# Graph layer with LayerNorm on one core: LayerNorm sums moved from ScalarE to VectorE, one rectification four tiles wide moved, other warming products

## The reference

```
h   = max((x - mean(x)) / sqrt(var(x) + 1e-5), 0)      x: 8192 x 128, mean and var over the 128 columns
out = x + relu(adj @ (h @ W) + b)                      adj: 8192 x 8192 dense float32, W: 128 x 128
```

## Time and profile before

| | |
|---|---|
| median of 3 runs | 722.23 us (722.19 to 722.49) |
| the profiled execution's own time | 722.6 us |
| its span | 720.8 us |
| PE, DVE, ACT, POOL busy | 99%, 86%, 72%, 24% of the span |
| transferred | 281.60 MB, mean 391 GB/s |

### The profile page before, as it was taken

One profiled execution on the slowest core, in us unless ns is written; L12 is line 12 of the kernel. 1 busy time (PEld: TensorE's weight loads), 2 busy tenths in 40 slices (PEclk: granted clock), 3 DMA queues, 4 the chain that ended last, 5 costly groups with the idle time before them and its releaser, 6 DMA issues.

```text
span 720.8 us, 7916 instructions
## 1 busy us (share of the span) xinstructions
PE 715.5 (99%) x3125; PEld 586.4 (81%) x3125; DVE 620.4 (86%) x387; ACT 517.0 (72%) x394; POOL 171.5 (24%) x99
## 2 busy tenths in 40 slices
PE   9999999999999999999999999999999999999998
PEld 5788888888888888888888888888888888888886
DVE  5899999999999888988789888878888787888885
ACT  2798988888888867766567677677676676766662
POOL 4445455554444402222011000000000000033213
PEclk9999999999999999999999999999999999999999
DMA  9999999999999999999999999999999999999992
GB/s 352 408 409 407 408 412 415 412 416 415 416 414 416 418 415 412 398 374 402 373 412 392 408 409 389 377 401 383 386 392 373 389 394 387 391 404 397 366 400 85
DMA packets 45109, 281.60 MB, mean 391 GB/s; under 512 B 5136, under 2 KB 5776, under 8 KB 31504
## 3 DMA queue, kind: packets, MB, share of 16 engines
q1 hardware_dynamic: 44496, 280.25, 97.5%
q10 hardware_dynamic: 576, 0.85, 0.4%
HBM read 276.89 MB, written 4.19 MB: 390 GB/s over the span
## 4 chain that ended last, share of the span: by engine, by line
PE 97%; DMA 2%; DVE 0%; ACT 0%; SPq 0%; issue 0%; DVEq 0%
PE banks L558 94%; DMA raw<-adj 2%; PE banks L600 2%; PE banks L592 1%; PE banks L585 0%; PE banks L586 0%; PE banks L584 0%; ACT high L378 0%; SPq L244 0%; DVE x_sb L479 0%; DVE x_sb L487 0%; DVEq L150 0%; DVE warm L491 0%; DVEq L478 0%
## 5 line engine op out<-in xcount | busy, mean ns | idle before, releaser
L516 DVE TENSOR_TENSOR low<-raw,high 128x3072 fp32r<-128x3072 f32 (+2 forms) x255 | 574.7, 2276 | 86.4 <-PE banks L558 64.4
L378 ACT ACTIVATE high<-raw 128x3072 fp32r<-128x3072 f32 (+2 forms) x255 | 483.0, 1903 | 190.3 <-DMA raw<-adj 178.4
L558 PE MATMUL banks<-high,h_high 128*128 128x512 f32 x1012 | 271.6, 390 | 1.1 <-ACT high L378 1.1
L558 PE MATMUL banks<-high,h_low 128*128 128x512 f32 x1012 | 271.0, 389 | 0.0
L558 PE MATMUL banks<-low,h_high 128*128 128x512 f32 x1012 | 267.8, 389 | 0.0
L558 PEld LDWEIGHTS banks<-high,h_high 128*128 128x128 f32 x1012 | 189.8, 188 | 41.8 <-ACT high L378 2.0
L558 PEld LDWEIGHTS banks<-low,h_high 128*128 128x128 f32 x1012 | 189.8, 188 | 39.9 <-DVE low L516 0.4
L558 PEld LDWEIGHTS banks<-high,h_low 128*128 128x128 f32 x1012 | 189.9, 188 | 39.5
L330 POOL TENSOR_SCALAR x_sb<-x_sb,bias 128x512 f32<-128x512 f32 x16 | 49.5, 3095 | 419.3 <-DMA x_sb<-x_blocks 419.3
L321 POOL TENSOR_SCALAR z_sb<-x_sb,neg_mean,rstd 128x128 f32<-128x128 f32 x60 | 89.8, 1510 | 1.6
L306 POOL TENSOR_TENSOR rstd<-var_eps,minus_half 128x4 f32<-128x4 f32 (+2 forms) x17 | 31.6, 1861 | 118.3 <-DVE var_eps L421 109.1
(11 more groups left out here) (34 smaller groups left out, 50.1 us busy)
## 6 DMA issues: line engine op xcount, KB each, us to landing
raw<-adj SPq DMA_DIRECT2D x106, 1536.0 KB, 8.9
raw<-adj SPq DMA_DIRECT2D x82, 768.0 KB, 10.5
raw<-adj SPq DMA_DIRECT2D x69, 512.0 KB, 11.8
x_sb<-x_blocks SPq DMA_DIRECT2D x16, 256.0 KB, 8.6
out_blocks<-x_sb SPq DMA_DIRECT2D x15, 256.0 KB, 9.7
x_sb<-x SPq DMA_DIRECT2D x14, 256.0 KB, 11.9
raw<-adj SPq DMA_DIRECT2D x3, 256.0 KB, 6.9
raw<-adj ACTq DMA_DIRECT2D x1, 256.0 KB, 2.7
```

What stands on the lines that cost most here:

```text
L378: nc.scalar.activation(high[:, t % HIGH_SLOTS, cols], raw[:, t % RAW_SLOTS, cols], ACT.Copy).then_inc(high_ready, 1)
L516: nc.vector.tensor_tensor(low[:, t % LOW_SLOTS, cols], raw[:, t % RAW_SLOTS, cols], high[:, t % HIGH_SLOTS, cols].bitcast(F32), ALU.subtra ...
L558: return nc.tensor.matmul(banks[:, FIRST_BANK[g] + c, :], h[:, (t - FIRST_STEP[g]) * DEPTHS[g] + k, :], tile[:, slot, at:at + BANK], start ...
```

## The change

All batches' sums are taken with bn_stats on DVE. From batch 4 on, one tile is summed at the end of each of four steps, the first of them the step at which the mean stood (load_step), and bn_aggr, var_eps and neg_mean follow the fourth. ACT's squares, DVE's mean and variance and their semaphores go. Batch 3 (tiles 8 to 11) is rectified at step 5 in place of step 7; all other rectifications keep their steps. The split of h_first moves from step 9 to step 28. The eight zero products of 128 columns become two of 448 columns, in memory shared with last_sum, which is filled by two memsets; PE waits for both, ACT for the first.

```diff
-SUMMED_BY_DVE = 4
+SUMMED_AHEAD = 4
...
-WARMING = 8
+WARMING, WARM = 2, 448
...
-def batch_at(t, phase, ahead):
-
-    j = t // 4 + ahead
-    return j if t >= FOUR_PASS and t % 4 == phase and j < len(BATCHES) else None
-
-
-def mean_at(t):
-    return batch_at(t, 1, 3) if t >= 5 else None
-
-
-def variance_at(t):
-    return batch_at(t, 3, 3) if t >= 7 else None
+def load_step(j):
+
+    return (j - 3) * 4 + 1
+
+
+def load_at(t):
+    return next((j for j in range(SUMMED_AHEAD, len(BATCHES)) if load_step(j) == t), None)
+
+
+def summed_at(t):
+
+    for j in range(SUMMED_AHEAD, len(BATCHES)):
+        if load_step(j) <= t < load_step(j) + 4:
+            return j, BATCHES[j][0] + t - load_step(j)
+    return None
 
 
 def rectified_at(t):
-    return 2 if t == 2 else batch_at(t, 3, 2) if t >= 7 else None
-
-
-def squares_at(t):
...
+
+    if t in (2, 5):
+        return 2 if t == 2 else 3
+    j = t // 4 + 2
+    return j if t % 4 == 3 and SUMMED_AHEAD <= j < len(BATCHES) else None
...
+        warm = last_sum[:, 0:WARM]
...
-                if mean_at(t) is not None:
-                    load_x(mean_at(t))
+                if load_at(t) is not None:
+                    load_x(load_at(t))
...
                 pool.wait_ge(rstd_ready, j + 1)
-                if j < SUMMED_BY_DVE:
-                    pool.wait_ge(centre_ready, j + 1)
+                pool.wait_ge(centre_ready, j + 1)
...
-            def square(j, tiles):
...
-                if squares_at(t) is not None:
-                    square(*squares_at(t))
...
-            def mean(j):
...
-            def variance(j):
...
+            def sums_of(j, t):
+                if t == BATCHES[j][0]:
+                    if j == 0:
+                        dve.wait_ge(x_first_landed, 16)
+                    else:
+                        dve.wait_ge(x_landed[x_slot(j)], x_landed_count(j))
+                cols = slice(t % 4 * P, t % 4 * P + P)
+                nc.vector.bn_stats(stats[:, t, :], x_sb[:, x_slot(j), cols]).then_inc(stats_ready, 1)
+
+            def moments_of(j):
                 first, end = BATCHES[j]
...
                 dve.wait_ge(stats_ready, end)
                 for t in range(first, end):
                     nc.vector.bn_aggr(moments[:, t, :], stats[:, t, :]).then_inc(moments_ready, 1)
...
+            def statistics(j):
+                for t in range(*BATCHES[j]):
+                    sums_of(j, t)
+                moments_of(j)
+
...
-            nc.vector.memset(warm[:, :], 0.0).then_inc(warm_ready, 1)
+            for cols in (slice(0, P), slice(P, WARM)):
+                nc.vector.memset(warm[:, cols], 0.0).then_inc(warm_ready, 1)
...
-                if mean_at(t) is not None:
-                    mean(mean_at(t))
-                if variance_at(t) is not None:
-                    variance(variance_at(t))
-                if t == 9:
+                if summed_at(t) is not None:
+                    j, tile = summed_at(t)
+                    sums_of(j, tile)
+                    if tile == BATCHES[j][1] - 1:
+                        moments_of(j)
+                if t == 28:
...
-            pe.wait_ge(warm_ready, 1)
+            pe.wait_ge(warm_ready, 2)
             for _ in range(WARMING):
-                nc.tensor.matmul(banks[:, PSUM_BANKS - 1, 0:P], warm[:, :], warm[:, :], start=True, stop=True)
+                nc.tensor.matmul(banks[:, PSUM_BANKS - 1, 0:WARM], warm[:, 0:P], warm[:, :], start=True, stop=True)
```

More of the change, by code:

```diff
@@ L51 @@
 ACT = mybir.ActivationFunctionType
-AXIS = mybir.AxisListType
 F32 = mybir.dt.float32
@@ L100, in landed @@
     return 16 * len([s for s in range(t % RAW_SLOTS, t + 1, RAW_SLOTS) if i < len(split_of(s))])
-def batch_at(t, phase, ahead):
-    j = t // 4 + ahead
-    return j if t >= FOUR_PASS and t % 4 == phase and j < len(BATCHES) else None
-def mean_at(t):
-    return batch_at(t, 1, 3) if t >= 5 else None
-def variance_at(t):
-    return batch_at(t, 3, 3) if t >= 7 else None
-def rectified_at(t):
-    return 2 if t == 2 else batch_at(t, 3, 2) if t >= 7 else None
-def squares_at(t):
[L123 to L127, removed]
+def load_step(j):
[7 more added lines that the diff above has]
+    return None
+def rectified_at(t):
+    if t in (2, 5):
+        return 2 if t == 2 else 3
+    j = t // 4 + 2
+    return j if t % 4 == 3 and SUMMED_AHEAD <= j < len(BATCHES) else None
 def x_slot(j):
@@ L163, in gnn_layer @@
         z_sb = sb("z_sb", [P, Z_SLOTS, BANK])
-        squares = sb("squares", [P, 4, P])
-        neg_sum = sb("neg_sum", [P, TILES])
         neg_mean = sb("neg_mean", [P, TILES])
-        sum_squares = sb("sum_squares", [P, TILES])
         var_eps = sb("var_eps", [P, TILES])
@@ L170, in gnn_layer @@
         rstd = sb("rstd", [P, TILES])
-        warm = sb("warm", [P, P])
         unread = sb("unread", [P, 1])
         h_first = sb("h_first", [P, FOUR_PASS, P])
-        stats = sb("stats", [P, BATCHES[SUMMED_BY_DVE - 1][1], 6])
-        moments = sb("moments", [P, BATCHES[SUMMED_BY_DVE - 1][1], 2])
+        stats = sb("stats", [P, TILES, 6])
+        moments = sb("moments", [P, TILES, 2])
         W_sb = sb("W_sb", [P, P])
@@ L199, in gnn_layer @@
         early_low = sem("early_low")
-        summed = sem("summed")
-        mean_ready = sem("mean_ready")
-        squared = sem("squared")
         var_ready = sem("var_ready")
@@ L404, in _ @@
         def _(dve):
-            def mean(j):
-                first, end = BATCHES[j]
[L407 to L416, removed]
-            def variance(j):
[L419 to L432, removed]
+            def sums_of(j, t):
[7 more added lines that the diff above has]
+            def moments_of(j):
+                first, end = BATCHES[j]
                 dve.wait_ge(stats_ready, end)
```

## The result

The changed kernel takes 738.66 us in the median of five runs (737.26 to 740.06), against 722.28 (722.19 to 722.49): a ratio of 1.0223, 95% interval 1.0212 to 1.0234, 16.4 us slower. The forecast was 721.9 us, no difference that can be measured. The profiled execution took 738.66 us, its span is 736.9 (before: 720.8).

The account below looks back on a forecast made before the run. PE was taken as the bound, busy 99% of the span. Gains of 0.36 and 0.29 less losses of 0.1 and 0.25 made 0.3 us off the median 722.23: 721.9 us, range 720.9 to 722.8.

Parts of the forecast that it names:

- The start, 0: New zero products at the start: done at 4.4 to 4.7 us, first real product at about 4.7 as now, 0.
- The wait at 30.49 us, 0.36 gained: PE's wait for step 5's late piece: likely moves to step 6's second piece; gain 0.36 us, bounds 0 and 1.1.
- Tiles 8 to 11 at step 5, 0: Rectifying these tiles at step 5, not 7, makes PE wait for nothing: 0, at most 0.3 us lost.
- over ten microseconds earlier: Step 5's rectification input: normalised that much ahead, even at POOL's slowest, so no wait.
- Step 9's split, 0.29 gained: h_first's conversion leaves step 9, ending PE's wait for DVE near 53 us: 0.29 us gained, bounds 0 and 0.35.
- step 28, 0.25 lost: h_first's split delays step 28's next subtraction; PE waits 0.1 to 0.4 us, taken as 0.25, bounds 0 and 0.6.
- Sums on DVE, 0: DVE's added bn_stats in narrow steps: 15.7 to 16.0 us of work against PE's 16.34 per four steps, so 0.
- 8.1 us: POOL's time for a batch's power and four normalisations, the mean over batches, expected unslowed by the added sums.
- The variance a step later, 0.1 given back: Variance after the fourth step, not third: ACT waits for POOL in step 27, PE loses 0.1 us near 122.
- Later batches have more room: After step 27, transfers and DVE gain on PE by some 0.3 us in four steps.
- Rival 3: POOL late at step 27, ACT waiting for z at L349: 10.3 us per batch, +1.7 us, 723.9; chance 0.10.
- the signs I had named for being wrong: Records of double length behind 4.7 us; PE waiting behind 135 us; POOL batches of over 9 us.

Follow-up runs that it names:

- the run with the two small moves: Kernel before with only tiles 8 to 11 rectified at step 5 and the split of h_first at step 28: 722.45 us (1.0001).
- the lump of the first step: Changed kernel with the eight old zero products and a batch's four bn_stats and moments together ending its first step: 723.86 us (1.0021).

## Why the prediction was wrong

**The start, 0:** right by size. The product began at 5.33 us in the profiled execution, not at 4.7: the first bn_stats waited for x until 3.37 us (2.54 in the run with the new zero products alone), and h_first was later for it. Five records ran at the lower clock's length. Two runs with the zero products exchanged show that neither reaches the end.

**The wait at 30.49 us, 0.36 gained:** the wait moved about as told, but no gain is seen. In five of the six profiled kernels with two zero products PE's wait for ACT stands at 34 to 35 us (0.15 to 0.94 us), in the changed kernel nowhere; in four of the six with eight it stands at 30 to 31 us. The profiled execution of the kernel before with two products is 0.4 us shorter (span 720.4), but the medians are equal. The instruction packet moved with it: it lies between 30 and 32 us in all six profiles with two zero products, and between 28 and 30 in five of the six with eight (in the sixth between 26 and 28). That it is the cause was not tested by itself.

**Tiles 8 to 11 at step 5, 0:** no wait of ACT for POOL is seen there, as forecast, but my "over ten microseconds earlier" was misread: in the changed kernel POOL is done with these tiles at 26.1 us and ACT comes to them at 30.27, 4.1 us later.

**Step 9's split, 0.29 gained, and step 28, 0.25 lost:** in the run with the two small moves the wait near 53 us went, and one near 108 us, with a transfer at its root, took its place; at step 28 PE doesn't wait. Net 0, for another reason than I gave.

**Sums on DVE, 0:** true of DVE's hours, false of what I took them for: with the variance as early as before they cost 8.4 us (730.68). I counted 15.7 to 16.0 us of work in 16.34 and called it fitting. I didn't count that the reduction of 0.68 us was also POOL's chance. In the kernel before, POOL and DVE of one round:

```profile
140.95 1.46 POOL L321 TENSOR_SCALAR z_sb<-x_sb,neg_mean,rstd 128x128 f32<-128x128 f32 x2
...
142.39 3.96 POOL L321 TENSOR_SCALAR z_sb<-x_sb,neg_mean,rstd 128x128 f32<-128x128 f32 x2
...
142.26 3.50 DVE L516 TENSOR_TENSOR low<-raw,high 128x1536 fp32r<-128x1536 f32 x2 [0.61 <-ACT high L378]
145.68 0.68 DVE L410 TENSOR_REDUCE neg_sum<-x_sb 128x4 f32<-128x512 f32 x1
```

Two normalisations pass in the 0.6 us in which DVE waits for ACT; the third is held for both subtractions and gets out 0.24 us into the reduction, and the fourth still fits into it, all by 146.35. In the changed kernel the pauses are bn_stats, each of which puts the next subtraction off by 0.2 us, and one normalisation passes at each:

```profile
169.02 4.54 POOL L312 TENSOR_SCALAR z_sb<-x_sb,neg_mean,rstd 128x128 f32<-128x128 f32 x2
...
173.54 2.50 POOL L312 TENSOR_SCALAR z_sb<-x_sb,neg_mean,rstd 128x128 f32<-128x128 f32 x2
...
169.84 3.47 DVE L482 TENSOR_TENSOR low<-raw,high 128x1536 fp32r<-128x1536 f32 x2
173.24 0.28 DVE L389 BATCH_NORM_STATS2 stats<-x_sb 128x6 f32<-128x128 f32 x1
...
173.63 1.74 DVE L482 TENSOR_TENSOR low<-raw,high 128x1536 fp32r<-128x1536 f32 x1
176.81 0.69 DVE L428 SCALAR_TENSOR_TENSOR h_low<-z_sb,h_high 128x512 fp32r<-128x512 f32 x1 [1.44 <-ACT h_high L329]
178.12 1.76 DVE L482 TENSOR_TENSOR low<-raw,high 128x1536 fp32r<-128x1536 f32 x1 [0.61 <-ACT high L357]
```

The second is held from 170.03 to 173.56. The Trainium skill (SBUF — State Buffer, the sections on the two separate sides and on who interferes with whom) names the lock: a DVE instruction with two inputs in SBUF holds the shared ports against a POOL instruction that reads SBUF; one with at most one input, outside the two-port modes, doesn't. The runs agree with that as far as they go: normalisations got out at a reduction and at a bn_stats (145.92 and 170.03 us above). From it I concluded that added one-input instructions slow nothing, and that 8.1 us would stand. The right reading was the other way round: beside back-to-back subtractions POOL gets little time, and the reduction that went was part of what it had. The form and place of DVE's pauses set how long a batch takes, though some normalisations get out between two subtractions as well.

**The variance a step later, 0.1 given back: this is the step that failed.** I followed one batch, from step 24's moments to step 27's subtraction, found it 0.1 us late, and wrote "Later batches have more room". I didn't follow on from that subtraction to the moments of step 28, which stand behind it on the same engine. With my own numbers the way closes: 8.1 for POOL, 4.0 to the end of step 27's subtraction, then two subtractions, 3.4, and 0.9 for the moments make 16.4 us, as much as PE's four steps. The ring was on the edge by the prediction's own terms, POOL's 9.6 us put it 1.45 us over, and being late once became being late ten times: 14.5 us in place of 0.1. By itself, in the kernel before, the later variance costs 10.2 us (732.45). Rival 3 named the place and the engine, and priced it as one delay of 1.7 us. Two of the signs I had named for being wrong came: PE waits behind 135 us, and POOL's batches take over 9 us.

## What to carry to other kernels

When a wait is added or a result comes later, follow it until the engine that produced it is reached again; if it is, what counts is the length of the whole round against the pace of the bound engine, and each round pays. A round's price isn't fixed: an engine that shares a resource with another member of it can get slower as soon as the round closes, so a shortening of one member may be eaten by another. And an engine's pauses can be another engine's working time; before removing them, look who gets through in them.

## What was unexpected of the hardware

- An added DVE instruction of 0.61 us in every fourth step made a kernel 7.1 us faster (730.68 to 723.55).
- A 128x128 normalisation on POOL took 0.44 us with DVE idle and up to 5.1 us beside DVE's back-to-back subtractions (in the lump of the first step, 137.28 to 142.40, where it got out between two of five subtractions in a row). A bn_stats between two subtractions, which put the second off by 0.2 us, let one through (in the changed kernel 0.24 to 0.32 us behind the end of the first):

```profile
137.28 5.11 POOL L312 TENSOR_SCALAR z_sb<-x_sb,neg_mean,rstd 128x128 f32<-128x128 f32 x1
...
137.06 8.61 DVE L481 TENSOR_TENSOR low<-raw,high 128x1536 fp32r<-128x1536 f32 x5
```

- Tensors and semaphores that nothing reads or waits for changed PE's pace around the projections by 0.56 us in 425.
- The number of real products that ran at the lower clock's length (0.853 us instead of 0.429) differed between executions: none to five with the two new zero products, none to three with the eight old ones.
